# A state-space scan spread over two stages: 24 of its 32 groups in the attention before, 8 in the feed-forward

## The reference, cut to what matters

```python
def step(state, inp):
    d, b, c, u = inp
    dA = jnp.exp(d[..., None] * A)
    state = state * dA + (d * u)[..., None] * b[:, None, :]
    y = jnp.einsum('bdn,bn->bd', state, c)
    return (state, y)
...
x = x + jnp.tanh(g_xattn[2]) * _L2_xattn_ref(_layernorm(x, axis=-1), ctx_1024, ...)
x = x + jnp.tanh(g_ffn[2]) * _L2_ffn_ref(_layernorm(x, axis=-1), ...)
x = x + jnp.tanh(g_xattn[3]) * _L3_xattn_ref(ctx_1024, _layernorm(x, axis=-1), ...)
```

## Time and profile before

| | |
|---|---|
| three runs | 1354.28, 1353.31, 1350.06 us; median 1353.31 |
| the profiled execution | 1356.47 us, its span 1354.7 us, mean granted clock of TensorE 0.903 |
| TensorE busy | 1097.0 us, 81% of the span |
| VectorE busy | 861.8 us, 64% |
| ScalarE busy | 666.9 us, 49% |
| GpSimd busy | 689.2 us, 51% |

### The profile page before, as it was taken

How to read it: one execution, slowest core, us unless ns; L and a number is a source line. 1 busy time by engine, 2 the same in 40 slices (tenths; PEclk the granted TensorE clock), 3 DMA queues, 4 the chain that set the end, 5 groups by cost and what they waited for, 6 DMA issues and landing times.

```text
span 1354.7 us, 18223 instructions
## 1 busy us (share of the span) xinstructions
PE 1097.0 (81%) x5412; PEld 845.8 (62%) x5413; DVE 861.8 (64%) x1512; ACT 666.9 (49%) x1705; POOL 689.2 (51%) x457
## 2 busy tenths in 40 slices
PE   6666598787635888999999999799999436999992
PEld 3445477666413555788888888655555335888782
DVE  3585998979669852466666665859996664332222
ACT  4392355544451113778778777467652115333330
POOL 1005888787611112245545445329984004888873
PEclk8878998999867998899999999989999658999996
DMA  6493899987520002111011110305445962555555
GB/s 178 139 176 91 226 251 287 264 239 164 94 70 0 1 1 90 49 52 49 23 51 53 49 51 1 98 1 144 145 137 107 273 173 55 82 81 83 81 81 128
DMA packets 141159, 146.19 MB, mean 108 GB/s; under 512 B 34197, under 2 KB 127374, under 8 KB 141078
## 3 DMA queue, kind: packets, MB, share of 16 engines
q1 hardware_dynamic: 115414, 110.58, 28.4%
q0 software_dynamic: 24576, 33.57, 14.8%
q10 hardware_dynamic: 1088, 1.05, 0.2%
HBM read 119.04 MB, written 26.12 MB: 107 GB/s over the span
## 4 chain that ended last, share of the span: by engine, by line
PE 47%; DVE 16%; issue 15%; POOL 11%; DMA 5%; ACT 5%; SPq 1%; DVEq 0%; POOLq 0%; ACTq 0%
PE bank L1496 4%; PE bank L1592 4%; PE bank L1559 4%; PE bank L1581 4%; PE bank L2347 3%; DVE arena L486 3%; PE bank L2024 3%; POOL y L2269 2%; PE bank L1485 2%; PE bank L1514 2%; PE bank L1570 2%; PE bank L989 2%; POOL arena L506 2%; PE bank L1286 2%; DMA e_sums<-ctxT,put 2%
## 5 line engine op out<-in xcount | busy, mean ns | idle before, releaser
L486 DVE TENSOR_TENSOR_SCAN arena<-arena 128x1024 f32<-128x1024 f32 x64 | 155.3, 2426 | 10.0 <-issue 5.1
L935 POOL DMA_INDIRECT f_sums<-arena,put x64 | 123.6, 1931 | 28.7 <-issue 16.8
L506 POOL TENSOR_TENSOR arena<-arena 128x1024 f32<-128x1024 f32 x32 | 82.5, 2577 | 92.6 <-DVE arena L486 92.6
L921 POOL DMA_INDIRECT arena<-y_rows,slots x64 | 83.2, 1299 | 71.2 <-DVEq L1130 52.0
L2260 POOL DMA_INDIRECT e_sums<-ctxT,put x64 | 101.6, 1588 | 26.5 <-issue 16.6
L2347 PE MATMUL bank<-arena,ssm_y 128*128 x512 | 111.7, 362 | 2.8 <-issue 1.1
L464 ACT ACTIVATE arena<-arena,ssm_A 128x255 f32<-128x255 f32 x256 | 107.9, 498 | 2.0 <-DVE arena L436 1.8
L2024 PE MATMUL bank<-yT,arena 128*128 128x512 f32 (+1 forms) x224 | 105.3, 616 | 2.2 <-ACT arena L1951 2.2
L516 PE MATMUL bank<-arena,ident 128*128 128x256 f32 x256 | 71.6, 428 | 37.8 <-DVE arena L506 33.3
L2269 POOL DMA_INDIRECT y<-y_rows,slots x64 | 64.4, 1007 | 68.5 <-DVEq L2508 49.3
L475 DVE TENSOR_TENSOR arena<-arena 128x1024 f32<-128x1024 f32 x64 | 93.8, 1466 | 1.3 <-DMA arena<-bc_rows 1.2
(11 more groups left out here) (328 smaller groups left out, 2757.2 us busy)
## 6 DMA issues: line engine op xcount, KB each, us to landing
arena<-bc_rows SPq DMA_DIRECT2D x64, 512.0 KB
arena<-in_L_ffn_w_gate_dram SPq DMA_DIRECT2D x16, 256.0 KB
arena<-in_L_ffn_w_up_dram SPq DMA_DIRECT2D x16, 256.0 KB
arena<-in_L_ffn_w_down_dram SPq DMA_DIRECT2D x16, 256.0 KB
x<-in_L_ffn_w_gate_dram SPq DMA_DIRECT2D x16, 256.0 KB
y<-in_L_ffn_w_up_dram SPq DMA_DIRECT2D x16, 256.0 KB
yT<-in_L_ffn_w_down_dram SPq DMA_DIRECT2D x16, 256.0 KB
arena<-in_L_ffn_Wd_dram SPq DMA_DIRECT2D x1, 3072.0 KB, 19.3
```

The source lines that it names most:

```text
L486: nc.vector.tensor_tensor_scan(ssm_h[:, j % 2, :], ssm_decay[:, j % 2, :], ssm_in, 0.0, ALU.mult, ALU.add).then_inc(s_ssm_h, 1)
L506: ops.tensor_tensor(ssm_hC_buf[:, j % 2, :], ssm_h[:, j % 2, :], ssm_C[:, g % 2, :], ALU.mult).then_inc(s_ssm_hC, 1)
L935: nc.gpsimd.indirect_dma_start(out=f0_sums[m % SUMS], out_offset=bass.IndirectOffsetOnAxis(ap=put[:, m:m + 1], axis=0), in_=f0_ye[:, n % R ...
```

## The change

Head h of the attention now carries a main group, and every odd head an extra one before it. The numbers run 0 | 1 2 | 3 | 4 5 | ..., so that heads 0 to 15 take groups 0 to 23. The extra group of odd head h has its exponentials at the end of step 3 of head h - 1, its product in step 0 and its scan in step 1 of head h, and its multiply and adds on GpSimd ahead of those of the main group. The loads of rows on SyncE, now 12 pairs, are issued before the weights of a head, as soon as the head's main group plus one reaches them. The sums of batch 0 come in step 1 of head 6, of batch 1 in step 2 of head 11, behind the q statistic. In the feed-forward 8 groups are left, one operation in each of steps 1 to 16: products in odd, scans in even steps. g_last becomes 16, and with it the early loads move from step 22 to step 17 of SyncE's list, and the last sums to step 18. The sums of batch 2 are at the start of the feed-forward.

```diff
+        XG = H + H // 2
+
+        def x_main(h):
+
+            return divmod(h + (h + 1) // 2, GB * HC)
+
+        def x_extra(h):
+
+            return divmod(h + (h + 1) // 2 - 1, GB * HC)
...
+            loads = collections.deque(range(0, XG, HC))
             for h in range(H):
-                if h % HC == 0:
-                    b, j = x_group(h)
+                while loads and loads[0] <= h + (h + 1) // 2 + 1:
+                    b, j = divmod(loads.popleft(), GB * HC)
                     ssm_load_sp(sp, 1, b, j // HC)
                 head(h // HB, h % HB)
...
                 if b == 1:
-                    ssm_act(act, 1, *x_group(i * HB + k))
+                    ssm_act(act, 1, *x_main(i * HB + k))
+                if b == 3 and k % 2 == 0:
+                    ssm_act(act, 1, *x_extra(i * HB + k + 1))
...
                 if b == 2:
-                    ssm_in_product(dve, 1, *x_group(h))
+                    ssm_in_product(dve, 1, *x_main(h))
                 elif b == 3:
-                    ssm_scan(dve, 1, *x_group(h))
+                    ssm_scan(dve, 1, *x_main(h))
+                elif k % 2:
+                    (ssm_in_product, ssm_scan)[b](dve, 1, *x_extra(h))
                 if ago >= 2:
                     add(s - 2, (b - 2) % B)
...
-                if b == 1 and h and x_group(h)[1] == 0:
-                    ssm_out_dve(dve, 1, x_group(h)[0] - 1)
+                if h and b == 1 and k % 2 == 0 and x_extra(h - 1)[1] == GB * HC - 1:
+                    ssm_out_dve(dve, 1, x_extra(h - 1)[0])
+                if h and b == 2 and x_main(h - 1)[1] == GB * HC - 1:
+                    ssm_out_dve(dve, 1, x_main(h - 1)[0])
...
-                ssm_out_pool(pool, 1, *x_group(h))
+                if k % 2:
+                    ssm_out_pool(pool, 1, *x_extra(h))
+                ssm_out_pool(pool, 1, *x_main(h))
...
-        XG = H
         g_work = [[] for t in range(STEPS)]
         pending = [(what, q) for q in range(XG, GROUPS) for what in ("product", "scan")]
         for t in range(1, STEPS):
-            share = 2 if t < 2 * SH else (2, 1, 1)[(t - 2 * SH) % 3]
+            share = 1
             g_work[t], pending = pending[:share], pending[share:]
```

More of the change, by code:

```diff
@@ L1 @@
+import collections
 from contextlib import ExitStack
@@ L1420, in after @@
                     eng.wait_ge(sem_, value)
-        def x_group(h):
-            return divmod(h, GB * HC)
+        XG = H + H // 2
[3 more added lines that the diff above has]
+            return divmod(h + (h + 1) // 2 - 1, GB * HC)
         def beyond(g):
```

## The result

| | kernel before | changed kernel |
|---|---|---|
| median (runs) | 1355.44 us (20) | 1359.05 us (20) |
| lowest to highest | 1349.23 to 1359.92 | 1351.2 to 1363.02 |
| profiled execution | 1356.47, span 1354.7 | 1355.9, span 1354.2 |

The ratio of the changed kernel to the one before is 1.003, with a 95% interval of 1.0016 to 1.0044: about 4 us slower, at the bound of what can be told from no change. The median is 4 us above the forecast 1355.0, at the upper end of the forecast's own range (1349 to 1359) and inside the wide one of 1346 to 1363. Of these 4 us, 2.1 are the base: over 20 runs the kernel before has a median of 1355.44, not 1353.31. In a second session the ratio was 1.0015 (0.9995 to 1.0035).

A forecast was written before the change was run, and what follows sets the result against it. TensorE was taken to bound the attention, VectorE and GpSimd's scan work the feed-forward. Attention +3.4 us less a feed-forward gain of 1.7 made +1.7, so 1355.0 us on a median of 1353.31; 8-in-10 range 1346 to 1363.

The forecast's parts named there:

- The feed-forward's gain: Layer 2's feed-forward: stalls of 13.3 us go, leaving 146.4 us from first down product to the last one's end.
- The feed-forward's loss: Feed-forward, step 22: row loads behind the early loads make TensorE stand about 9.1 us, clock 2.2; only 1.7 gain left.
- the late end: Feed-forward: latest landing of chunk 8's row load, behind the early loads, near 1028.5 us; 1026.5 was taken.
- the early end: Feed-forward: earliest landing of chunk 8's row load, at once on its issue near 1020.6 us.
- The attention: Layer 2's attention: the added groups cost 0.6 + 1.4 + 1.4 = +3.4 us (1 to 7).
- The six ordinary odd heads: Attention, heads 1, 3, 5, 7, 9 and 13: a copy in step 2 about 0.1 us late each, 0.6 in all.
- Head 11: Attention: batch 1's sums make step 2's copy 0.7 us late and put the scan behind GpSimd's multiply; together 1.4 us.
- Heads 14 and 15: Attention's end: head 15's late step 1 copy costs 1.1 us, step 3 up to 0.5; 1.4 taken.
- The sum: Whole kernel: 3.4 us attention loss less 1.7 us feed-forward gain, +1.7 us; 1355.0 on the median of 1353.31.
- The first: Rival, feed-forward: row loads aren't late; up to −9.9 us, 1343.4, or partly, −6, 1347; chance together 0.19.
- The second: Rival, attention: GpSimd's multiply beats the scan in step 3 of every odd head; +7.3 to +11.5, near 1362.5; chance 0.25.
- The third: Rival: pauses of 0.3 to 0.5 us in odd heads and 11 us at the rows; +5 to +8, 1359; chance 0.09.

The follow-up runs named there:

- wd17: The changed kernel with only the 3072 KB early load at step 17 and the other early loads at step 22; 1352.47 us, ratio 0.9924 to the kernel before.
- early22: The changed kernel with the early loads of layer 3's weights back at step 22, behind the last row loads; 1349.72 us, ratio 0.9924 to the kernel before.
- early22_scanlate: The changed kernel with early loads at step 22 and each head's step 3 scan moved behind VectorE's add to x; 1354.17 us, ratio 0.996.
- rows_act: The changed kernel, early loads still at step 17, with the row loads of chunks 8 to 10 issued by ScalarE instead of SyncE; 1347.53 us, ratio 0.991.
- rows_act_out12: The changed kernel with ScalarE issuing the row loads of chunks 8 to 10 and batch 1's sums in step 0 of head 12; 1344.17 us, ratio 0.993.
- the repeat: The changed kernel run once more, unaltered, beside the kernel before, with a second profile; 1364.32 us, ratio 1.0015.
- early22_share2: The changed kernel with early loads at step 22 and the old sharing rule in the feed-forward, two operations in each of steps 1 to 5; 1355.49 us, ratio 0.9958.

## Why the prediction was right, by its steps

**The feed-forward's gain** was 13.3 us, an undisturbed stage of 146.4 to the end of the last product. Measured without the pause: 13.4 and 144.57 + 1.73 = 146.3. The extra work fits.

**The feed-forward's loss** had the right mechanism, and it is the term of the sum that was mis-sized. In times of before (3.71 us earlier than in the changed kernel, by the first down product), the loads start at 994.4 (forecast 994.5) and hold SyncE 26.1 us (26.1). Then the forecast let the rows land 5.9 us after their issue, at 1026.5; VectorE went on at 1029.2, 8.7 us after issue: the first row load's own issue was held 1.5 us, which the sum had at nothing, and the second landed 7.1 us behind that. The choice between 1020.6 and 1028.5 was too early by 2.7, the landing is 0.6 us behind even the late end, and nothing of the early end showed. So TensorE stood 11.95 us, not 9.1: beyond the 11.1 given as the end. From the end of the pause to the start of the last product it is 26.39 us (1034.37 to 1060.76), against 23.65 before: the clock cost 2.7 us, not 2.2. Of 13.3 us nothing was left: −1.6 instead of +1.7. The Trainium skill's sentence on the order of completion (DMA: Bandwidth & Descriptors, "Queues, rings and completion order") doesn't promise the early end: the same section says that each DMA engine takes the descriptors of a ring in their order. The wd17 run agrees with that, its rows came 2.3 us behind the large load ahead of them.

**The attention** was forecast at +3.4 us in three terms. The six ordinary odd heads cost nothing instead of 0.6: they start every 20.54 us, as before. The chain was met closely: the scaling ends at 581.57 in times of before (forecast 581.6), the product is held up by it (2.65 us, has 1.20), the scan starts at 584.81 (584.9), GpSimd's multiply 0.37 us later (0.45). Only the copy of step 2 ends at 583.84 and not 583.94, and TensorE wanted it at 584.02. Head 11 cost 1.44 us (1.4): TensorE idles 0.41 us for the copy behind the sums and 0.50 us behind the scan of 4.33 us. Heads 14 and 15 cost 1.9 (1.4). The idle time that TensorE has in them beyond before's is 0.38 us in head 14, which the forecast had left out, and 0.78 and 0.48 in head 15. So the good sum hides two errors that cancel, 0.6 too much and 0.5 too little. Sum to the last projection +3.3, and +3.1 to the first down product.

**The sum**: +3.1 + 1.6 = +4.6 us against +1.7. Both parts kept their mechanism, so that the total is no luck, though its error (2.9 us) is larger than the change forecast; 3.3 us of error lie at the row loads and the clock behind them, where the trace of before had shown no such order of loads.

**The rivals.** The first (rows not late) fell with the pause of 12 and 13 us in two profiles; early22 shows what it would have been worth. The second (the multiply beats the scan) was decided by 0.37 us in six heads and went the forecast's way; in head 11 it came true, as forecast. The prediction priced it at 7.3 − 1.7 = 5.6 to 9.8 us beyond the sum. early22_scanlate cost 3.0, but with a multiply 0.7 us ahead and with the add out of the scan's way, so that price is not tested. The third named nearly the measured time, by pauses in odd heads that are not there.

## What to carry to other kernels

When a step is moved in an engine's issue list, write down what now stands behind it in the same queue and when each of those is wanted: here early loads that nobody needed for a while took back a gain of 13 us, and putting them back, or giving the small urgent loads to another engine's queue, restored it. Where two engines exclude each other, find the lead of the one over the other in the trace; a few tenths decide, and the price is what is left of the instruction in the way, less what slack the work behind the delayed one has. Measure a small repair at the next stage's start, not at the stall removed: of 1.4 us in head 11 1.2 came back, and of 3.0 in heads 11 and 15 together 2.7.

## What the runs showed of the hardware

- Loads issued on one queue came behind the bytes in front of them: in wd17 the rows were there 20.7 us after their first issue began, 6.9 of them a held issue, and 2.3 us behind the load of 3072 KB that took 18.8. On ScalarE's queue the row loads took 6.7 to 10.5 us beside the same traffic (rows_act and rows_act_out12).
- SyncE was held 26.1 us by the six early loads at step 17, as at step 22 before; 26.8 to 29.7 us in the repeat, in early22 and in the two kernels with the rows on ScalarE.
- What a pause of TensorE costs in the matmuls behind it is not a function of its length: 2.7 and 2.2 us behind 12.0 and 13.0 us, but 1.8 us behind one pause of 2.20 us (before, granted clock 0.72 in the three us around it) and 0.1 us behind another of 2.20 us (early22_share2, clock 1.00).
- With head 11's 1.4 us removed, the clock fell sooner some 80 us later: the last projection took 2.08 us in place of 1.13, in both runs of that kernel, and 2.07 in rows_act_out12. In both runs with a shorter head 15 the router's matmuls took 7.00 us, not 4.8. Why stays open.
